# Moving one group of products and replacing one: messages between the first norm's transposes and the queries, and own squares as rows of the distance product

## The reference, cut to what matters

```
# layer 0
s    = x @ w_se.T + b_se                       # 3 values per node
sq   = sum(s*s)                                # "own square" of a node
dist = sq[n] + sq[m] - 2 * s[n].s[m]           # 512 x 512
A    = exp(-dist)
msg  = relu(x @ w_msg.T + b_msg)
x_nmp  = A @ msg ;  x_conv = 17-tap convolution over the nodes
x1   = layernorm(GRU(x_conv, x_nmp, x))        # "first norm"
# layer 1
q, k, X = leaky(x1 @ W_q), leaky(x1 @ W_k), leaky(x1 @ W_lin + b)
att  = sigmoid(q @ k.T * scale) ; ...
```

## Time and profile before

| What | Value |
|---|---|
| median of three runs | 773.96 us (771.95 to 775.07) |
| the profiled execution | 773.77 us, span 772.0 us |
| TensorE busy | 709.7 us, 92% of the span |
| VectorE busy | 625.5 us, 81% |
| ScalarE busy | 423.6 us, 55% |
| GpSimd busy | 138.0 us, 18% |
| mean granted TensorE clock | 0.976 |

### The profile page before, as it was taken

How to read it: one execution, slowest core, us unless ns; L and a number is a source line. 1 busy time by engine, 2 the same in 40 slices (tenths; PEclk the granted TensorE clock), 3 DMA queues, 4 the chain that set the end, 5 groups by cost and what they waited for, 6 DMA issues and landing times.

```text
span 772.0 us, 12824 instructions
## 1 busy us (share of the span) xinstructions
PE 709.7 (92%) x3984; PEld 547.4 (71%) x3984; DVE 625.5 (81%) x2080; ACT 423.6 (55%) x881; POOL 138.0 (18%) x151
## 2 busy tenths in 40 slices
PE   3879999999999999999999999999999999998553
PEld 1757877777787867777787867778687777775531
DVE  7456788888888888888888888888888888876655
ACT  4153754747374665748375665738465565734431
POOL 0000121221121111122121111112121121111221
PEclk9999999999999999999999999999999999998886
DMA  5304333150614233160513234060523324101000
GB/s 204 123 0 134 113 110 110 65 182 14 207 39 149 82 122 122 34 211 14 183 62 128 103 110 135 16 228 14 177 68 119 112 81 164 56 15 55 5 10 28
DMA packets 46585, 75.33 MB, mean 98 GB/s; under 512 B 4064, under 2 KB 12768, under 8 KB 46432
## 3 DMA queue, kind: packets, MB, share of 16 engines
q1 hardware_dynamic: 46560, 75.02, 28.9%
HBM read 70.82 MB, written 4.19 MB: 97 GB/s over the span
## 4 chain that ended last, share of the span: by engine, by line
PE 81%; ACT 10%; DVE 5%; issue 3%; POOL 1%; DMA 0%; SPq 0%; ACTq 0%; POOLq 0%; DVEq 0%
PE K L1267 11%; PE C L1395 7%; PE F L1403 7%; PE C L1327 7%; PE K L1432 7%; PE CONV L1300 6%; PE K L1300 6%; PE F L1327 6%; ACT JUNKD L487 5%; PE K L1260 4%; PE C L1267 3%; ACT A L454 3%; PE K L1381 2%; PE K L1287 2%; PE F L1383 2%
## 5 line engine op out<-in xcount | busy, mean ns | idle before, releaser
L337 POOL TENSOR_TENSOR RSTD<-VEPS,POW 128x4 f32<-128x4 f32 x48 | 48.9, 1019 | 276.7 <-DVE VEPS L687 276.7
L1300 PE MATMUL CONV<-H1H,WH 128*128 128x256 f32 x288 | 84.5, 293 | 0.0
L1300 PE MATMUL CONV<-H1L,WH 128*128 128x256 f32 x288 | 81.7, 284 | 0.0
L1300 PE MATMUL CONV<-H1H,WL 128*128 128x256 f32 x288 | 81.4, 283 | 0.0
L1395 PE MATMUL C<-QT,KT 128*128 128x512 f32 x128 | 62.0, 609 | 0.0
L1267 PEld LDWEIGHTS K<-XS,BIG 128*128 128x128 f32 x496 | 57.8, 192 | 1.3
L1267 PE MATMUL K<-XS,BIG 128*128 128x128 f32 x496 | 57.9, 275 | 0.0
L1403 PE MATMUL F<-A,MSG 128*128 128x512 f32 x128 | 57.6, 592 | 0.0
L1300 PEld LDWEIGHTS CONV<-H1L,WH 128*128 128x128 f32 x288 | 55.4, 192 | 0.6
L1300 PEld LDWEIGHTS CONV<-H1H,WH 128*128 128x128 f32 x288 | 55.3, 192 | 0.7
L1300 PEld LDWEIGHTS CONV<-H1H,WL 128*128 128x128 f32 x288 | 55.3, 192 | 0.0
(11 more groups left out here) (262 smaller groups left out, 1966.1 us busy)
## 6 DMA issues: line engine op xcount, KB each, us to landing
ADJF<-in_adjT SPq DMA_DIRECT2D x16, 1024.0 KB, 5.3
ADJN<-in_adj SPq DMA_DIRECT2D x16, 1024.0 KB, 7.6
ADJM<-in_adjT SPq DMA_DIRECT2D x15, 1024.0 KB, 5.6
ADJR<-in_adjT SPq DMA_DIRECT2D x14, 1024.0 KB, 5.2
X_IN<-in_xT SPq DMA_DIRECT2D x16, 256.0 KB, 2.6
out<-OUT SPq DMA_DIRECT2D x16, 256.0 KB, 2.7
BIG<-in_weights SPq DMA_DIRECT2D x1, 1088.0 KB, 5.2
BIG<-in_weights SPq DMA_DIRECT2D x1, 576.0 KB, 9.0
```

The source lines that it names most:

```text
L337: nc.gpsimd.tensor_tensor(RSTD[:, row, :], VEPS[:, row, :], POW[:, 0, :], ALU.pow).then_inc(ev[f"ln{layer}_rstd"], 1)
L1300: last = mm(out, w[:, at_col + k * P:at_col + (k + 1) * P], h[:, k:k + PH], start=(k == 0 and i == 0), stop=(k == count - 1 and i == 2))
```

## The change

The bias b_se now comes in by a product of its own (`SEH`, two rows, times a tile of ones, `ONER`), so that K0 holds s itself. The columns of w_se are repeated at 32 to 43 as well, and ScalarE squares these twelve rows (rows 32 to 63 of K0) in place. The stacks take the squares as further rows, against rows of ones, so the product with SQMAT is gone, and `parts` waits for the squaring alone. SQMAT's transfer (64 KB) becomes a transfer of SE (1 KB); the start gains one fill and two small VectorE operations that split SE. The order of TensorE's steps changes: the messages and the first norm's transposes now stand directly ahead of the projections. No other engine's order changes.

```diff
@@ ScalarE
             def squares(count):
                 act.wait_ge(ev["g1_done"], count)
-                A(SQ[:, :], K0[:, :], ACT.Square, bias=PAR[:, SQ_BIAS:SQ_BIAS + 1]).then_inc(ev["sq_ready"], 1)
+                A(K0[SQUARES:2 * SQUARES, :], K0[SQUARES:2 * SQUARES, :], ACT.Square).then_inc(ev["sq_ready"], 1)
             def parts(count):
-                act.wait_ge(ev["g_done"], count)
+                act.wait_ge(ev["sq_ready"], count)
@@ VectorE, start
+            V.memset(ONER[:, :].bitcast(F32), 1.0)
...
+            V.tensor_scalar(SEZ[:, :], SE[:, :], PAR[0:2, SE_LEFT:SE_LEFT + 1], None, ALU.mult).then_inc(s_se, 1)
+            dve.wait_ge(s_se, 1)
+            V.tensor_tensor(SEH[:, :], SE[:, :], SEZ[:, :].bitcast(F32), ALU.subtract).then_inc(s_se, 1)
@@ TensorE
             def factors(count, previous):
                 pe.wait_ge(ev["xl"], count)
                 pe.wait_ge(ev["xconv_part"], previous)
-                product(K0[:, :], [(weight(W_SE), (XH[:, :], XL[:, :]))]).then_inc(ev["g1_done"], 1)
-
-            def own_squares(count):
-                pe.wait_ge(ev["sq_ready"], count)
-                mm(K0[:, :], SQMAT[:, :], SQ[:, :], start=False, stop=True, skip_group_check=True).then_inc(
-                    ev["g_done"], 1)
+                mm(K0[:, :], SEH[:, :], ONER[:, :], start=True, stop=False)
+                for k, (w, x) in enumerate(((WH, XH), (WH, XL), (WL, XH))):
+                    last = mm(K0[:, :], w[:, W_SE:W_SE + P], x[:, :], start=False, stop=(k == 2))
+                last.then_inc(ev["g1_done"], 1)
@@ TensorE, body of a slot (the ending alike)
                 if mid:
                     state_by_nodes(n)
-                    messages(n)
                 distances(n)
-                if not mid:
-                    messages(n)
                 first_taps(n)
-                if mid:
-                    first_norm_by_features(n)
                 even_taps(8, EVEN)
                 if n["first"]:
                     pe.wait_ge(s_split, 3)
                 odd_taps(0, 2)
+                if mid:
+                    first_norm_by_features(n)
+                messages(n)
                 if mid:
                     projections(n)
...
                 update_gate(n)
-                if following:
-                    own_squares(n["f_next"])
                 new_gate(n)
```

More of the change, by code:

```diff
@@ L45 @@
 (G1, B1, M1, V1, G2, B2, M2, V2, BI_R, BI_Z, BI_N, BH_R, BH_Z, BH_N,
- SQ_BIAS, L_A, L_ZA, L_ZC, R_A, R_ZA, R_ZC) = range(21)
+ SE_LEFT, L_A, L_ZA, L_ZC, R_A, R_ZA, R_ZC) = range(21)
 N_PAR = 21
+SQUARES = 32
 EVENTS = (
@@ L54 @@
     "gatez_done r_ready w_ready gate_t gate_u n_ready gate_x gate_e y_ready x_used gater_done "
-    "a0_ready g1_done conv1_done msg_done g_done conv2_done agg0_done gates_done yt_done x1_ready "
+    "a0_ready g1_done conv1_done msg_done conv2_done agg0_done gates_done yt_done x1_ready "
     "x1t_done x1t_ready x_done q_done k_done q_raw k_raw x_raw q_ready k_ready xact_ready "
@@ L66, with adj_resnorm_kernel @@
 DMA_EVENTS = "x_loaded adjf_loaded adjm_loaded adjr_loaded adjn_loaded mask_loaded out_stored".split()
-def adj_resnorm_kernel(nc, xT_d, adjT_d, adj_d, mask_d, weights_d, less_d, rows_d, params_d, sqmat_d, ident_d, out_d):
+def adj_resnorm_kernel(nc, xT_d, adjT_d, adj_d, mask_d, weights_d, less_d, rows_d, params_d, se_d, ident_d, out_d):
     ctx = ExitStack()
@@ L86, in adj_resnorm_kernel @@
         PAR = sb("PAR", [P, N_PAR])
-        SQMAT = sb("SQMAT", [P, P])
+        SE = sb("SE", [2, P])
+        SEZ, SEH = sb("SEZ", [2, P], F32R), sb("SEH", [2, P], F32R)
+        ONER = sb("ONER", [2, N], F32R)
         IDENT = sb("IDENT", [P, P])
@@ L107, in adj_resnorm_kernel @@
         XT, XH, XL = sb("XT", [P, N]), sb("XH", [P, N], F32R), sb("XL", [P, N], F32R)
-        SQ = sb("SQ", [P, N])
         ZL, ZR = sb("ZL", [P, N], F32R), sb("ZR", [P, N], F32R)
@@ L166, in adj_resnorm_kernel @@
         s_set, s_bn_pow, s_bn, s_less = sem("s_set"), sem("s_bn_pow"), sem("s_bn"), sem("s_less")
+        s_se = sem("s_se")
         def at(e, t, k):
@@ L260, in _ @@
             sp.dma_start(PAR[:, :], params_d).then_inc(s_const, 16)
-            sp.dma_start(SQMAT[:, :], sqmat_d).then_inc(s_const, 16)
+            sp.dma_start(SE[:, :], se_d).then_inc(s_const, 16)
             sp.dma_start(IDENT[:, :], ident_d).then_inc(s_const, 16)
@@ L1273, in _ @@
             pe.wait_ge(s_set, 4)
+            pe.wait_ge(s_se, 2)
             def first_conv(count, previous):
@@ L1282, in factors @@
                 pe.wait_ge(ev["xconv_part"], previous)
-                product(K0[:, :], [(weight(W_SE), (XH[:, :], XL[:, :]))]).then_inc(ev["g1_done"], 1)
-            def own_squares(count):
-                pe.wait_ge(ev["sq_ready"], count)
-                mm(K0[:, :], SQMAT[:, :], SQ[:, :], start=False, stop=True, skip_group_check=True).then_inc(
-                    ev["g_done"], 1)
+                mm(K0[:, :], SEH[:, :], ONER[:, :], start=True, stop=False)
+                for k, (w, x) in enumerate(((WH, XH), (WH, XL), (WL, XH))):
+                    last = mm(K0[:, :], w[:, W_SE:W_SE + P], x[:, :], start=False, stop=(k == 2))
+                last.then_inc(ev["g1_done"], 1)
             first_conv(1, 0)
             factors(1, 0)
-            own_squares(1)
             xt, xc, nm = (XH[:, :], XL[:, :]), (XCH[:, :], XCL[:, :]), (NMH[:, :], NML[:, :])
@@ L1517, in ending @@
                 state_by_nodes(a)
-                messages(a)
                 distances(a)
                 first_taps(a)
-                first_norm_by_features(a)
                 even_taps(8, EVEN)
                 odd_taps(0, 2)
+                first_norm_by_features(a)
+                messages(a)
                 projections(a)
@@ L1563, in packed @@
     w_se = zeros((P, P), np.float32)
-    for g in range(3):
-        w_se[:, 5 * g:5 * g + 3] = t(i["L0_gnn_w_se"])
+    for at_col in (0, 3, 6, *range(32, 44, 3)):
+        w_se[:, at_col:at_col + 3] = t(i["L0_gnn_w_se"])
     conv2 = np.asarray(i["L0_gnn_conv2_w"]).transpose(1, 2, 0)
@@ L1584, in packed @@
         par[:, k:k + 3] = t(np.asarray(i["L0_gnn_" + name]).reshape(3, P))
[L1587 to L1600, removed]
+    par[1, SE_LEFT] = 1
+    se = zeros((2, P), np.float32)
+    for at_col in (0, 3, 6, *range(32, 44, 3)):
+        se[:, at_col:at_col + 3] = i["L0_gnn_b_se"]
+    par[0:9, L_A], par[0:9, R_A] = 1, 2
+    par[3:6, L_ZA], par[6:9, R_ZA] = 1, 2
+    par[32:38, L_A], par[35:38, L_ZA], par[32:38, R_ZC] = 1, 1, 1
+    par[38:44, R_A], par[41:44, R_ZA], par[38:44, L_ZC] = 1, 1, 1
     c = np.ascontiguousarray
@@ L1605, in packed @@
         "mask": c(np.asarray(i["nodemask"])[:, nodes].reshape(B, C, P).transpose(0, 2, 1)), "weights": c(weights),
-        "less": c(less), "rows": c(rows), "params": par, "sqmat": sqmat, "ident": np.eye(P, dtype=np.float32),
+        "less": c(less), "rows": c(rows), "params": par, "se": se, "ident": np.eye(P, dtype=np.float32),
     }
```

## The result

The changed kernel takes 772.25 us (median of 20 runs, 770.68 to 773.33) against 774.19 us (20 runs, 771.15 to 776.03) for the kernel before: ratio 0.9975, 95% interval [0.9965, 0.9986]. It is 0.25% faster, clear of the noise, where 1.2% was forecast; it lies outside the range of 759 to 770. It is also under the 0.5% that the prediction asks for before it says "faster", so by its own bar the outcome is "the same", to which it gave 0.15. The profiled execution is the shortest of the 20, 770.68 us with a span of 768.9, so in the two traces the difference is 3.1 us and in the medians 1.9.

A forecast was written before the change was run, and what follows sets the result against it. TensorE (92% busy) looked like the bound, with Y, X1T and KT nearly as late. From 773.8 us: +1.0 for squares and Y, -6.3 for the loop's reordering, -3.9 at the start, giving 764.6 us; range 759 to 770.

The forecast's parts named there:

- The bounds named: Three places in a loop slot, Y, X1T and KT, where another engine is nearly as late as TensorE.
- Own squares removed: Factors: squares' 0.86 us goes, added product costs 0.23; TensorE saves 0.63 a slot, but Y comes 0.07 later, +1.0 us.
- ZL's wait: On the chain to Y: ZL's 0.17 us wait for the own squares goes.
- The head of the slot: Y's transposes to attention: of X1T's 0.55 us wait, 0.28 is lost to KT and 0.27 kept.
- KT's 0.58 us to spare: Before the attention: VectorE ends KT at 320.03, TensorE starts at 320.61; 0.25 of this margin is used.
- The attention: Attention's 3.70 us in each slot: the first sigmoid is no longer late for the third chunk, gain 0.2 us.
- The start: Slot 0: taps fill the 3.95 us wait for WF; A x MSG starts at 28.0 instead of 31.96, -3.9 us.
- Rival 1: Loop gives nothing: VectorE's and ScalarE's losses to later messages and Y eat the 0.47 us; 769.9 us, chance 0.14.
- Rival 2: Whole kernel: TensorE's work is all that counts, 24.9 us saved, 749 us; chance 0.05.
- Rival 3: Loop slots: VectorE's wait for the messages makes it slower; 1.0 us later MSG gives 778.6 us; chance 0.05.
- Rival 4: Slot 0: split pieces or the low clock keep the taps from filling the wait; 768.5 us, chance 0.08.

The follow-up runs named there:

- e3: Changed kernel with the bias product (SEH, ONER) over all 128 rows, zeros in the weights below the second: 764.95 us, ratio 0.9879.
- e4: Changed kernel with the two-row bias product issued twice, ONER set to 0.5: 775.89 us, ratio 1.0033.
- e9: Changed kernel with the bias product over 32 rows instead of two, zeros in the added weights: 771.85 us, ratio 0.9967.
- e10: Changed kernel with the bias product over 64 rows instead of two, zeros in the added weights: 771.23 us, ratio 0.9960.
- e2_order_only: Kernel before with its old squares and TensorE's new order of steps: 766.95 us, ratio 0.9907.
- e1: Changed kernel (new squares) with TensorE's old order of steps: 780.12 us, ratio 1.0071.
- e11: e3 with the first norm's transposes back ahead of the last nine taps: 776.22 us, ratio 1.0023.

## Why the prediction was wrong, step by step

**The bounds named** (Y, X1T, KT) were right: X1T's wait went, and waits for Y and KT appeared (0.61 and 0.30, against 0.7 and "short"). That Y's has nearly the size forecast is luck. The forecast was 0.63 of TensorE's work saved and Y 0.07 later; measured are 0.86 - 0.62 = 0.24 saved and Y 0.33 later.

**The step that failed** is "Own squares removed": "No row has a product over two partitions: I take 0.23 for it, with nothing as the lower bound and the fp32 half-product, 0.43, as the upper." It costs 0.62, above the upper bound. e3, e4, e9 and e10 show that the change of height does it, and the rows of the weight loads suggest how: two of them no longer start with the product before. Y moved by +0.33 instead of +0.07, in 15 slots 3.9 us. The bound was taken from products that all had 128 rows, so it could not hold a cost that lies between unlike neighbours. The Trainium skill (TensorE: Matmul & The Clock Gate, "Why this matters for your kernels"), put beside that step, says that a single product over 32 rows takes as long as one over 128. Of a series of mixed heights that row of the page says nothing: in e9_rows32 one over 32 rows among products over 128 costs 0.62 us against 0.23, and its own row is 0.49 long against 0.39.

**ZL's wait** of 0.17 went as said. The step from WG to ZL is 0.10 shorter still, which was not forecast. ScalarE's rows suggest why: where nothing is waited for, a row starts about 0.1 before the end of the one before (H1H, 0.78 long, is followed 0.68 after its start), and a row that waits does not. No run tries this.

**The head of the slot** gave 0.24 of 0.27, by two errors that cancel. Counted from Y's transposes, MSG comes 0.18 later than before and KT only 0.09 later, not 0.25 both. But the attention starts 0.24 after KT's end (317.20 to 317.44), where the prediction took 0.06; so KT's 0.58 us to spare was nearer 0.34. Why this handover takes longer than Y's 0.06 is open.

**The attention.** The first sigmoid's gain was over-valued: 0.07 instead of 0.2, 14 times, 1.8 us. The sigmoid stood 1.23 us after the attention's start and now stands 318.60 - 317.44 = 1.16 after it. It can't come sooner, for ScalarE now waits 0.29 us for TensorE's first chunk; it had been late by 0.07 only. In e3_full_height the loss of 1.8 us and the 0.10 a slot above nearly cancel, which is why that kernel, which has the product as I priced it, ends at 764.95 us, beside the forecast of 764.6. So the sum was right for that kernel, partly by luck: by these two small errors of opposite sign.

**The start** gave 3.8 of 3.9 us; the clock rose near 21.7 us (the taps' distance falls from 0.21 to 0.12 there), where I had taken 22. At slot 1's transposes 0.7 us is gone again: 0.33 is the two-row product in slot 0; the rest, some 0.4, shows as H1L starting late on VectorE. From A x MSG to these transposes it is 20.6 us in the kernel before, in e2_order_only and in e3_full_height, 21.3 in the changed kernel, 21.0 in e9_rows32 and 22.6 in e10_rows64. So the rest is not a fixed price of the short product; its cause is open.

**The sum with measured terms:** -3.8 + 0.4 + 15 x 0.33 - 14 x 0.31 = -2.8 us, against 3.1 between the traces. Counted by the starts of Y's transposes, the changed kernel is 3.1 ahead in slot 1, 2.7 in slot 2, 3.0 in slot 4, 2.6 in slot 15 after eleven loop slots, and 3.1 at the last.

**The rivals.** Rival 1 (the loop gives nothing) is what happened, with Y as the eater, as it says; it had 0.14 and 769.9 us. The profiled execution is 0.8 above that, about what the start lost again by slot 1. Its condition, "what VectorE and ScalarE lose", did not name the product that makes them late. Rival 2 is excluded: in e1, TensorE has 0.24 us less work a slot and the slot is 0.33 longer, because Y is last. Rival 3's mechanism did not act in the change, but it is what e11 shows: a wait for X1 in front of the transposes, 0.65 us a slot, goes with 11 us in all. The margin that kept it away was 0.3 us. Rival 4 did not come.

## What to carry to other kernels

Where several engines arrive within tenths of a microsecond of each other once per loop, a saving on the busiest one can be worth nothing; list every such meeting with its spare time, and price an edit by what it does to the later of the two. A term that no row shows, on the side that ends last, deserves a bound from unlike neighbours too: a run with the one operation swapped (full height instead of two rows) found 7 us here. Each filled wait should be checked for what else it had been hiding. Where a row starts late, look at the weight loads too: they showed here what the products' rows alone did not.

## What the runs showed of the hardware that was not expected

A matmul over 2, 32 or 64 rows among matmuls over 128 rows (fp32r, 512 columns, at the full clock) costs about 0.62 us instead of 0.23 (changed kernel, e9_rows32, e10_rows64): it starts 0.32 or 0.33 after the one before, the next one 0.42 or 0.43 after it, and the second next 0.34 after that. Its weight load and the next one's start with their own products, where a load in the same series with 128 rows throughout (e3_full_height) starts with the product before. Two matmuls over two rows, one behind the other, start 0.33 apart (e4_two_halves). ScalarE's square over 32 rows, in place in PSUM and without a bias tile, takes 0.56 us, against 0.69 for the one over 128 rows with a bias tile into SBUF.
